# Scales of the last eight quads by way of ScalarE and GpSimd, in a GRU with block attention

## The chip, the cores and the metric

One core of one Trainium2 chip. The metric is the device time of one execution in microseconds; three runs of the kernel before took 367.89, 368.22 and 368.25 us, median 368.22 us.

## The reference, cut to what matters

```
x = x + GRU(initial_state=cond, inputs=x)           # 32 sequences b, 64 steps t, 512 channels
# layer 1, with the blocks of 8 steps summed to 8 keys per sequence:
attn     = softmax(scores of the 8 block sums)      # one weight per block
attended = sum over blocks of attn * block sum      # one vector per b
y        = x + attended @ Wo.T                      # the same vector cp for every t of one b
out      = x + (y - mean(y)) / sqrt(var(y) + 1e-6) * ln_gamma + ln_beta
```

The variance of `y` over the 512 channels of a token is taken from three parts: the sum of squares of the centred `x` (`s2`), twice the product of `x` with the centred `cp`, summed over the channels (the cross sum), and a constant per sequence from `cp` alone (`cp_const`, which holds epsilon too). The scale of a token is that sum to the power -0.5.

## The kernel before, in words

The 64 steps are taken in 16 quads of 4 steps (`Q` = 4, `NQ` = 16); 4 steps by 32 sequences fill the 128 partitions. Up to 336 us the core runs the recurrence, with the input projections of later quads between the steps. Behind the last step comes the tail of some 28 us to which the change belongs: the last block's key and weight, `cp`, and then for each quad one row of output. Every engine has its own program, in order, and the semaphores (`wait_ge`, `then_inc`) tie them together; nothing reorders them.

The quads' scales are computed in three parts (`parts_i`, L114): part 0 holds quads 0 to 3, part 1 quads 4 to 7, part 2 quads 8 to 15. For each part:

- TensorE, `cross_sums` (L771): 16 matmuls per four quads into a bank (`cross_ps[part]`; `keys_ps` for part 2, 128x256).
- VectorE, `cross_own_sums` (L1187): one instruction takes two times the bank by the mask `tok_of_b` (own sequence only), a reduction sums over b. `cross_part` (L1204): that sum by `inv_d` plus `s2` gives `var`.
- ScalarE, `root` (L568): square root with the bias `cp_const`.
- VectorE, `inverse` (L1213) and `spread_rstd` (L213): reciprocal, and the scales spread by the mask into `rstd_of`.
- TensorE, `lay_rstd` (L782): turns the scales into a column per quad (`fourth_ps`), which ScalarE, `keep_rstd` (L576), copies to `rstd_tok`; `add_gcp` (L790) adds the scaled `cp` to the output banks, and needs `rstd_of` too.

For each quad TensorE transposes `x` into an output bank (`lay_x1`, L715; six banks in turn, so quad q waits until VectorE has finished quad q-6), and VectorE's `finish` (L1221) computes the output row in `gcx`, waiting for `u_laid` (the bank is complete) and `rstd_kept`. SyncE stores each row (L324 to L327).

The order of the tail on TensorE is written out in L799 to L839: part 2's cross sums, `lay_s2`, quads 4 and 5, `lay_rstd(1)`, quads 6 and 7, `add_gcp(1)`, quads 8 and 9, `lay_rstd(2)`, quads 10 and 11, `add_gcp(2)`, and so on. That of VectorE stands in L1230 to L1255: `finish(0)` to `finish(3)`, then part 2's scales, `centre_tokens(15)`, then `finish(4)` to `finish(15)`. ScalarE's is in L583 to L593. GpSimd has nothing after its last power, L384.

```
            finish(3)
            cross_own_sums(2)
            cross_part(2)
            inverse(2)
            spread_rstd(dve, 2)
            centre_tokens(NQ - 1)
            for quad in range(Q, NQ):
                finish(quad)
```

Of the kernel before, what the change touches and what calls it, by code (L numbers as in the profile page):

```python
# [8 lines left out]
ALU = mybir.AluOpType  # L9
# [4 lines left out]
P = 128  # L14
# [10 lines left out]
def gru_block_attention(nc, x_tok_d, x_t_d, cond_d, w_ih_d, w_hh_d, bias_d, recs_d, rows_d, wk_t_d,  # L25
# [3 lines left out]
    with ctx:  # L29
# [6 lines left out]
        def sem(name):  # L36
            return ctx.enter_context(nc.semaphore(name))
# [124 lines left out]
            sem("gcp_laid"), sem("gcp_kept"), sem("cross_laid"), sem("cross_step"))  # L162
        var_ready, std_ready, rstd_ready, rstd_spread, rstd_laid, rstd_kept = (
            sem("var_ready"), sem("std_ready"), sem("rstd_ready"), sem("rstd_spread"), sem("rstd_laid"), sem("rstd_kept"))
        u_laid, out_ready, out_stored = sem("u_laid"), sem("out_ready"), sem("out_stored")

        def wait(eng, s, value):
# [45 lines left out]
        def spread_rstd(eng, part):  # L213

            owns = parts_i[part]
            cols, size = slice(owns[0] * Q, (owns[-1] + 1) * Q), len(owns)
            mask = tok_of_b[:].rearrange("p (b t) -> p b t", t=Q)[:, None].broadcast_to([P, size, B, Q])
            scale = rstd[:, cols].rearrange("p (i t) -> p i t", i=size)[:, :, None].broadcast_to([P, size, B, Q])
            eng.tensor_tensor(rstd_of[:, owns[0] * P:(owns[-1] + 1) * P].rearrange("p (i b t) -> p i b t", i=size, t=Q),
                              mask, scale, ALU.mult).then_inc(rstd_spread, 1)  # L220

        block = ctx.enter_context(nc.Block())

# [107 lines left out]
        @block.gpsimd  # L331
        def _(pool):
            pool.memset(bias_rows, 0.0).then_inc(bias_cleared, 1)
            pool.memset(own_rows, 0.0).then_inc(own_made, 1)
            own = own_rows[0:2 * NJ, :].rearrange("p (j b) -> p j b", j=NJ)
            for half_ in range(2):

                pool.wait_ge(own_made, 1 + half_)
                pool.affine_select(out=own, in_=own, compare_op=ALU.not_equal, fill=1.0, base=-NJ * half_,
                                   pattern=[[-1, NJ], [0, B]], channel_multiplier=1).then_inc(own_made, 1)  # L340
            pool.wait_ge(own_made, 3)
            pool.memset(ident[:], 0.0).then_inc(made, 1)
            pool.memset(same_b[:], 0.0).then_inc(made, 1)
            pool.memset(tok_of_b[:], 0.0).then_inc(made, 1)
            pool.memset(own_n[:], 0.0).then_inc(made, 1)
            pool.memset(half[:], -0.5).then_inc(made, 1)
            pool.memset(key_ss[:], 0.0).then_inc(made, 1)
            pool.memset(key_dot[:], 0.0).then_inc(made, 1)
            pool.memset(sums_of, 1.0).then_inc(made, 1)

            pool.wait_ge(made, 8)
            pool.affine_select(out=ident[:], in_=ident[:], compare_op=ALU.not_equal, fill=1.0, base=0,
                               pattern=[[-1, P]], channel_multiplier=1).then_inc(made, 1)
            for g in range(NJ):
                rows = slice(g * B, (g + 1) * B)
                v = same_b[rows, :].rearrange("p (j b) -> p j b", j=NJ)
                w = tok_of_b[rows, :].rearrange("p (b t) -> p b t", t=Q)

                pool.wait_ge(made, 9 + 3 * g)
                pool.affine_select(out=v, in_=v, compare_op=ALU.not_equal, fill=1.0, base=0,  # L360
                                   pattern=[[0, NJ], [-1, B]], channel_multiplier=1).then_inc(made, 1)
                pool.wait_ge(made, 10 + 3 * g)
                pool.affine_select(out=w, in_=w, compare_op=ALU.not_equal, fill=1.0, base=0,
                                   pattern=[[-1, B], [0, Q]], channel_multiplier=1).then_inc(made, 1)
                pool.wait_ge(made, 11 + 3 * g)
                pool.memset(own_n[rows, g:g + 1], 1.0).then_inc(made, 1)

            def save_block(nb):

                wait(pool, br_ready, nb + 1)  # L370
                pool.tensor_copy(br_all[:, bass.ds(nb * P, P)], br_cur[:])
                pool.tensor_copy(br_t[:, :, bass.ds(nb * B, B)],
                                 br_turned[:].rearrange("p (k b) -> p k b", k=NJ)).then_inc(br_saved, 1)

            with pool.Fori(1, NB) as i:
                save_block(i - 1)

            for group in range(2):

                pool.wait_ge(key_var_ready, group + 1)  # L380
                pool.tensor_tensor(key_rms[:, group:group + 1], key_ss[:, group:group + 1], half[:, 0:1], ALU.pow
                                   ).then_inc(key_rms_ready, 1)
            pool.wait_ge(last_var_ready, 1)
            pool.tensor_tensor(last_rms, last_var, half[:, 0:1], ALU.pow).then_inc(last_rms_ready, 1)  # L384
        @block.scalar
        def _(act):
            def split_x(quad):
# [48 lines left out]
            def token_stats(quad, trash=third_ps[:]):  # L436

                wait(act, x1_ready, quad + 1)
                act.activation(trash, gcx_of(quad), ACT.Copy, scale=-1.0 / D, accum_out=column(x_mean, quad)
                               ).then_inc(mean_ready, 1)  # L440
                wait(act, mean_ready, quad + 1)
                act.activation(trash, gcx_of(quad), ACT.Square, bias=column(x_mean, quad),
                               accum_out=column(s2_tok, quad)).then_inc(s2_ready, 1)
# [124 lines left out]
            def root(part):  # L568

                owns = parts_i[part]  # L570
                cols = slice(owns[0] * Q, (owns[-1] + 1) * Q)
                act.wait_ge(cp_const_ready, 1)
                act.wait_ge(var_ready, part + 1)
                act.activation(rstd[:, cols], var[:, cols], ACT.Sqrt, bias=cp_const[:, 0:1]).then_inc(std_ready, 1)
# [11 lines left out]
            keep_rstd(0)  # L586
            root(1)
            token_stats(NQ - 1, stats_trash)
            act.wait_ge(s2_laid, 2)
            move_s2(NQ - Q, Q, fourth_ps, 4 * Q)  # L590
            keep_rstd(1)
            root(2)
            keep_rstd(2)  # L593

        @block.tensor
        def _(pe):
# [184 lines left out]

            def lay_rstd(part):  # L782

                pe.wait_ge(rstd_spread, part + 1)
                for i in parts_i[part]:
                    mm = pe.matmul(fourth_ps[:, P + i * Q:P + (i + 1) * Q], rstd_of[:, i * P:(i + 1) * P],
                                   own_n[:], start=True, stop=True, skip_group_check=True)
                mm.then_inc(rstd_laid, 1)
# [53 lines left out]
        def _(dve):  # L842
# [344 lines left out]
            def cross_own_sums(part):  # L1187

                owns = parts_i[part]
                cols = slice(owns[0] * Q, (owns[-1] + 1) * Q)  # L1190
                size = len(owns)
                own = cross_own[:, 0:size * P]
                dve.wait_ge(cross_laid, part + 1)
                wait(dve, cross_step, 2 * part)
                dve.scalar_tensor_tensor(out=own.rearrange("p (i c) -> p i c", i=size),
                                         in0=cross_ps[part][:, 0:size * P].rearrange("p (i c) -> p i c", i=size),
                                         scalar=2.0, in1=tok_of_b[:, None, :].broadcast_to([P, size, P]),
                                         op0=ALU.mult, op1=ALU.mult).then_inc(cross_step, 1)
                dve.wait_ge(cross_step, 2 * part + 1)
                dve.tensor_reduce(cross[:, cols].rearrange("p (i t) -> p i t", i=size),  # L1200
                                  own.rearrange("p (i b t) -> p i t b", i=size, t=Q), AX.X, ALU.add
                                  ).then_inc(cross_step, 1)

            def cross_part(part):  # L1204

                cols = slice(parts_i[part][0] * Q, (parts_i[part][-1] + 1) * Q)
                dve.wait_ge(cross_step, 2 * part + 2)
                dve.wait_ge(s2_moved, (1, 1, 2)[part])
                dve.wait_ge(denom_step, 3)
                dve.scalar_tensor_tensor(out=var[:, cols], in0=cross[:, cols], scalar=inv_d, in1=s2[:, cols],  # L1210
                                         op0=ALU.mult, op1=ALU.add).then_inc(var_ready, 1)
# [34 lines left out]
            split_s2(NQ - Q, NQ)  # L1246
            finish(2)
            finish(3)
            cross_own_sums(2)
            cross_part(2)  # L1250
            inverse(2)
            spread_rstd(dve, 2)
            centre_tokens(NQ - 1)
            for quad in range(Q, NQ):
                finish(quad)  # L1255
# [46 lines left out]
```

## Time and profile before

| | |
|---|---|
| median of 3 runs | 368.22 us (367.89 to 368.25) |
| the profiled execution, its own time | 368.15 us |
| its span, first to last instruction | 366.3 us |
| granted TensorE clock, mean | 1.0 |
| TensorE busy | 358.6 us, 98% of the span |
| VectorE busy | 263.6 us, 72% |
| ScalarE busy | 166.4 us, 45% |
| GpSimd busy | 11.7 us, 3% |

The profiled execution took 1.85 us more than its span (368.15 against 366.3); this lies around the instructions. Times in the rows are counted from the start of the span. In a row of a timeline stand the start, the time from the first to the last record of the group, the engine, the line of the kernel, the operation, the tensor written and those read, the shape, and the count; in square brackets stands the idle time of the engine before it and what ended it. `gcx` holds the output rows; the tail's small tensors (`cross_own`, `rstd_of`, `var`) lie inside `w_hh`, which the recurrence no longer needs, and `s2` inside `b_in`, so the rows name these.

### The profile page before, as it was taken

What the parts mean: (1) busy time and instruction counts of PE and PEld (TensorE: products, weight loads), DVE (VectorE), ACT (ScalarE), POOL (GpSimd) and SP (SyncE); (2) the same over time, 40 slices, a digit from 0 to 9 for tenths busy, and PEclk for the clock granted to TensorE, in tenths of its full rate; (3) what the DMA queues carried; (4) which work ended last, traced back from release to release, by engine and by line L of the source; (5) the groups of instructions that cost most, each with busy time, mean ns of one, the idle gap of its engine ahead of it and who ended that gap; (6) DMA issues with size and microseconds to landing.
All of it is one profiled execution on the core that took longest, in us unless ns stands there. A gap on an engine that the chain in (4) does not pass through costs nothing.

```text
span 366.3 us, 9562 instructions
## 1 busy us (share of the span) xinstructions
PE 358.6 (98%) x3096; PEld 185.4 (51%) x3096; DVE 263.6 (72%) x1129; ACT 166.4 (45%) x525; POOL 11.7 (3%) x46
## 2 busy tenths in 40 slices
PE   8999999999999999999999999999999999999995
PEld 4545555444555544555544555544555544434772
DVE  3827767677777767776768767776867676888886
ACT  4852236252625343442626262534445255857430
POOL 6000000000000000000000000000000000000000
PEclk9999999999999999999999999999999999999999
DMA  7952625323232322223132323232222312211138
GB/s 309 420 185 73 195 93 166 91 64 88 86 86 86 86 72 72 86 60 112 43 100 57 86 86 86 84 88 64 77 88 57 111 42 69 71 29 30 31 140 320
DMA packets 36275, 38.35 MB, mean 105 GB/s; under 512 B 3992, under 2 KB 27672, under 8 KB 36256
## 3 DMA queue, kind: packets, MB, share of 16 engines
q1 hardware_dynamic: 36240, 38.09, 33.5%
q8 instruction: 11, 0.18, 0.2%
q14 instruction: 8, 0.07, 0.1%
q10 hardware_dynamic: 16, 0.02, 0.0%
HBM read 17.91 MB, written 4.19 MB: 60 GB/s over the span
## 4 chain that ended last, share of the span: by engine, by line
PE 86%; DMA 5%; DVE 3%; issue 3%; SPq 1%; ACT 0%; DVEq 0%; POOLq 0%; POOL 0%; ACTq 0%
PE gates_ps L648 43%; PE gi_ps L616 36%; DMA w_hh<-in_w_hh_dram 2%; DMA gcx<-in_w_ih_dram 2%; PE gi_ps L630 1%; PE fourth_ps L648 1%; PE third_ps L648 1%; PE keys_ps L648 1%; DMA h_tok<-hist 1%; PE gi_ps L729 1%; DVE gcx L1226 0%; PE small_ps L795 0%; SPq L283 0%; DVEq L29 0%; PE small_ps L729 0%
## 5 line engine op out<-in xcount | busy, mean ns | idle before, releaser
L648 PE MATMUL gates_ps<-w_hh,turned 128*32 128x384 f32 x1920 | 167.3, 489 | 0.4 <-DVE turned L875 0.3
L648 PEld LDWEIGHTS gates_ps<-w_hh,turned 128*32 128x32 f32 x1920 | 56.4, 109 | 90.5 <-issue 48.8
L493 ACT ACTIVATE rz<-gates_ps 128x256 f32<-128x256 f32 x59 | 22.7, 384 | 129.1 <-PE gates_ps L648 129.1
L616 PE MATMUL gi_ps<-w_ih_hi,xt_hi 128*128 128x512 f32 x180 | 76.4, 427 | 0.0
L616 PE MATMUL gi_ps<-w_ih_lo,xt_hi 128*128 128x512 f32 x180 | 70.5, 394 | 0.0
L616 PE MATMUL gi_ps<-w_ih_hi,xt_lo 128*128 128x512 f32 x180 | 69.5, 389 | 0.0
L937 DVE TENSOR_TENSOR rz<-gates_ps,rz 128x128 f32<-128x128 f32 x59 | 17.2, 291 | 72.1 <-ACT rz L493 72.0
L616 PEld LDWEIGHTS gi_ps<-w_ih_hi,xt_hi 128*128 128x128 f32 x180 | 33.6, 187 | 42.3 <-issue 36.8
L616 PEld LDWEIGHTS gi_ps<-w_ih_hi,xt_lo 128*128 128x128 f32 x180 | 33.8, 188 | 7.7
L875 DVE STREAM_TRANSPOSE turned<-hist 128x32 f32<-128x32 f32 x189 | 36.1, 216 | 2.1
L616 PEld LDWEIGHTS gi_ps<-w_ih_lo,xt_hi 128*128 128x128 f32 x180 | 33.8, 188 | 5.4 <-issue 0.6
L869 DVE TENSOR_TENSOR hist<-zh,n 128x32 f32<-128x32 f32 x189 | 33.6, 201 | 2.5 <-DVE n L862 0.2
L854 DVE TENSOR_TENSOR gi_tok<-gi_ps,b_in 128x512 f32<-128x512 f32 x45 | 30.7, 683 | 0.0
L862 DVE SCALAR_TENSOR_TENSOR n<-rz,n 128x32 f32<-128x32 f32 x189 | 30.4, 188 | 0.0
L502 ACT ACTIVATE n<-n 128x32 f32<-128x32 f32 x126 | 28.5, 257 | 2.2 <-DVE n L944 1.7
L417 ACT ACTIVATE gates_ps<-bhh_n 128x128 f32<-128x128 f32 x60 | 16.9, 282 | 21.4 <-DVE rz L937 21.4
L426 ACT ACTIVATE gates_ps<-gi 128x256 f32<-128x256 f32 x60 | 22.2, 370 | 0.0
L944 DVE TENSOR_TENSOR n<-rz,gi 128x32 f32<-128x32 f32 x118 | 21.3, 222 | 0.4
L453 ACT ACTIVATE x1t<-x1t,beta_t (+1 forms) x64 | 20.2, 386 | 0.0
L881 DVE TENSOR_TENSOR x1t<-x1t,turned 128x512 f32 (+1 forms) x15 | 16.5, 1103 | 1.9
L945 DVE TENSOR_TENSOR zh<-rz,hist 128x96 f32<-128x96 f32 x63 | 15.8, 251 | 0.0
L391 ACT ACTIVATE xt_hi<-x1t 128x512 fp32r (+1 forms) x15 | 9.4, 629 | 9.0 <-PE gi_ps L616 9.0
(232 smaller groups left out, 295.8 us busy)
## 6 DMA issues: line engine op xcount, KB each, us to landing
gi<-gi_tok SPq DMA_DIRECT2D x60, 128.0 KB, 3.0
x1t<-in_x_t_dram SPq DMA_DIRECT2D x16, 256.0 KB, 2.7
gcx<-in_x_tok_dram SPq DMA_DIRECT2D x16, 256.0 KB, 2.8
h_tok<-hist SPq DMA_DIRECT2D x64, 64.0 KB, 2.1
out_dram<-gcx SPq DMA_DIRECT2D x16, 256.0 KB, 2.1
gi<-gi_tok SPq DMA_DIRECT2D x60, 64.0 KB, 2.2
gcx<-in_w_ih_dram SPq DMA_DIRECT2D x4, 768.0 KB, 6.7
w_hh<-in_w_hh_dram SPq DMA_DIRECT2D x4, 768.0 KB, 9.4
```

The source lines that it names most:

```text
L426: act.activation(gates_ps[:, P:3 * P], gi[:, (s // Q) % 2, first + P:first + G3], ACT.Copy).then_inc(seeded, 1)
L453: ins = act.activation(tile[:, k, :], tile[:, k, :], ACT.Identity, bias=beta_t[:, k * B:k * B + 1])
L493: act.activation(rz[:], gates_bank(t)[:, P:3 * P], ACT.Sigmoid).then_inc(rz_ready, 1)
L502: act.activation(n[:, c], n[:, c], ACT.Tanh).then_inc(n_ready, 1)
L616: mm = pe.matmul(gi_ps[tok][:], a[:, k, :], chunk_cols(w[:, k, :], c), start=(m % 12 == 0), stop=(m % 12 == 11))
L648: mm = pe.matmul(gates_bank(t)[j * B:(j + 1) * B, P:], before[:, k * B:(k + 1) * B], chunk(w_hh, k, j), start=False, stop=(k == NJ - 1), s ...
L854: dve.tensor_tensor(chunk_rows(gi_tok[:, tok, :], c), chunk_rows(gi_ps[tok][:], c), chunk_cols(b_in[:], c), ALU.add).then_inc(gi_tok_ready, 1)
L862: dve.scalar_tensor_tensor(out=n[:, c], in0=z[:, c], scalar=1.0, in1=n[:, c], op0=ALU.subtract, op1=ALU.mult).then_inc(terms_ready, 1)
L869: dve.tensor_tensor(hist[:, s, c], zh[:, c], n[:, c], ALU.subtract).then_inc(h_ready, 1)
L875: dve.transpose(turned[:, s, c], hist[:, s, c]).then_inc(ht_ready, 1)
L937: dve.tensor_tensor(r, bank[:, 3 * P:], r, ALU.mult).then_inc(rh_ready, 1)
L944: dve.tensor_tensor(n[:, c], r[:, c], i_n[:, c], ALU.add).then_inc(n_pre_ready[number], 1)
```

## The change

Parts 0 and 1 stay as they are. For part 2 (quads 8 to 15) the work is laid out anew:

- ScalarE copies the bank of cross sums, by 2, into `cross_own[:, P:3P]` in SBUF (`late_copied`), in its program behind the sums of squares of the last quad and ahead of the move of `s2`.
- GpSimd multiplies it by the mask in place (128x256), adds `cp_const` to `s2` into `var` (128x8), and after VectorE's sums takes the power -0.5 of `cross` into `rstd` (128x8) and spreads it into `rstd_of` (128x256, `late_spread`).
- VectorE keeps the sum over b (`tensor_reduce`, `late_summed` 1) and one instruction, `cross * inv_d + var` (`late_summed` 2). Its product with the mask, its reciprocal and its spread go.
- ScalarE's `root(2)` goes. TensorE's `lay_rstd(2)` waits for `late_spread`.

```diff
@@ gpsimd @@
             pool.tensor_tensor(last_rms, last_var, half[:, 0:1], ALU.pow).then_inc(last_rms_ready, 1)
+
+            late_own, late_cols = cross_own[:, P:3 * P], slice(2 * Q, 4 * Q)
+            pool.wait_ge(late_copied, 1)
+            pool.tensor_tensor(late_own.rearrange("p (i c) -> p i c", i=2), late_own.rearrange("p (i c) -> p i c", i=2),
+                               tok_of_b[:, None, :].broadcast_to([P, 2, P]), ALU.mult).then_inc(late_step, 1)
+            pool.wait_ge(s2_moved, 2)
+            pool.wait_ge(cp_const_ready, 1)
+            pool.tensor_tensor(var[:, late_cols], s2[:, late_cols], cp_const.broadcast_to([P, 2 * Q]), ALU.add
+                               ).then_inc(late_step, 1)
+            pool.wait_ge(late_summed, 2)
+            pool.tensor_tensor(rstd[:, late_cols], cross[:, late_cols], half[:], ALU.pow).then_inc(late_step, 1)
+            pool.wait_ge(late_step, 3)
+            spread_rstd(pool, 2)
@@ scalar @@
             token_stats(NQ - 1, stats_trash)
+            act.wait_ge(cross_laid, 3)
+            act.activation(cross_own[:, P:3 * P], cross_ps[2][:, 0:2 * P], ACT.Copy, scale=2.0).then_inc(late_copied, 1)
             act.wait_ge(s2_laid, 2)
             move_s2(NQ - Q, Q, fourth_ps, 4 * Q)
             keep_rstd(1)
-            root(2)
             keep_rstd(2)
@@ tensor, lay_rstd @@
-                pe.wait_ge(rstd_spread, part + 1)
+                if part == 2:
+                    pe.wait_ge(late_spread, 1)
+                else:
+                    pe.wait_ge(rstd_spread, part + 1)
@@ vector @@
             finish(3)
-            cross_own_sums(2)
-            cross_part(2)
-            inverse(2)
-            spread_rstd(dve, 2)
+            dve.wait_ge(late_step, 1)
+            dve.tensor_reduce(cross[:, 2 * Q:4 * Q].rearrange("p (i t) -> p i t", i=2),
+                              cross_own[:, P:3 * P].rearrange("p (i b t) -> p i t b", i=2, t=Q), AX.X, ALU.add
+                              ).then_inc(late_summed, 1)
+            dve.wait_ge(late_summed, 1)
+            dve.wait_ge(late_step, 2)
+            dve.scalar_tensor_tensor(out=cross[:, 2 * Q:4 * Q], in0=cross[:, 2 * Q:4 * Q], scalar=inv_d,
+                                     in1=var[:, 2 * Q:4 * Q], op0=ALU.mult, op1=ALU.add).then_inc(late_summed, 1)
             centre_tokens(NQ - 1)
```

VectorE's program before, from `finish(3)` to `finish(5)` (L1226 is `finish`, L898 `centre_tokens`):

```order
L1226 SCALAR_TENSOR_TENSOR gcx<-gcx,w_hh,gi_ps 128x512 [waits rstd_kept,u_laid,gcx_ready]
L1195 SCALAR_TENSOR_TENSOR w_hh<-keys_ps,tok_of_b 128x256 [waits cross_step,cross_laid]
L1200 TENSOR_REDUCE w_hh<-w_hh 128x8 [waits cross_step]
L1210 SCALAR_TENSOR_TENSOR w_hh<-w_hh,b_in 128x8 [waits denom_step,s2_moved,cross_step]
L1218 RECIPROCAL w_hh<-w_hh 128x8 [waits std_ready]
L219 TENSOR_TENSOR w_hh<-tok_of_b,w_hh 128x256 [waits rstd_ready]
L898 SCALAR_TENSOR_TENSOR gcx<-gcx,x_mean,tok_consts 128x512 [waits s2_ready]
L1226 SCALAR_TENSOR_TENSOR gcx<-gcx,w_hh,gates_ps 128x512 [waits rstd_kept,u_laid,gcx_ready]
```

and with the change (line numbers of the changed file: L1246 is `finish`, L918 `centre_tokens`):

```order
L1246 SCALAR_TENSOR_TENSOR gcx<-gcx,w_hh,gi_ps 128x512 [waits rstd_kept,u_laid,gcx_ready]
L1270 TENSOR_REDUCE w_hh<-w_hh 128x8 [waits late_step]
L1275 SCALAR_TENSOR_TENSOR w_hh<-w_hh 128x8 [waits late_step,late_summed]
L918 SCALAR_TENSOR_TENSOR gcx<-gcx,x_mean,tok_consts 128x512 [waits s2_ready]
L1246 SCALAR_TENSOR_TENSOR gcx<-gcx,w_hh,gates_ps 128x512 [waits rstd_kept,u_laid,gcx_ready]
```

Five instructions between two outputs' finishes and ahead of `centre_tokens` became two. They wait for GpSimd (`late_step`) in place of TensorE's bank and ScalarE's root.

GpSimd's program from its first power to its end, with the change (before, it ended with the row of L386):

```order
L383 TENSOR_TENSOR b_in<-key_ss,half 128x1 [waits key_var_ready] x2
L386 TENSOR_TENSOR w_hh<-w_hh,half 128x1 [waits last_var_ready]
L390 TENSOR_TENSOR w_hh<-w_hh,tok_of_b 128x256 [waits late_copied]
L394 TENSOR_TENSOR w_hh<-b_in,w_hh 128x8 [waits cp_const_ready,s2_moved]
L397 TENSOR_TENSOR w_hh<-w_hh,half 128x8 [waits late_summed]
L221 TENSOR_TENSOR w_hh<-tok_of_b,w_hh 128x256 [waits late_step]
```

The last four are new; the third of them is a power over eight columns, and the last one is what `lay_rstd(2)` waits for.

## Rows read from the trace of the kernel before

**Rows 1.** The page, part 4: the chain that ended last, shares of the span by engine.

```profile
PE 86%; DMA 5%; DVE 3%; issue 3%; SPq 1%; ACT 0%; DVEq 0%; POOLq 0%; POOL 0%; ACTq 0%
```

**Rows 2.** The chain that ended last, in order of time: start us, us, what.

```profile
355.79 0.66 PE gates_ps L729 x4
...
356.45 0.66 PE gi_ps L729 x4
...
361.63 0.66 DVE gcx L1226
```

**Rows 3.** Timeline of VectorE (DVE): start us, us, engine, line, operation, out<-in, count.

```profile
351.34 0.74 DVE L1226 SCALAR_TENSOR_TENSOR gcx<-gcx,w_hh,gi_ps 128x512 f32<-128x512 f32 x1
351.99 0.42 DVE L1195 SCALAR_TENSOR_TENSOR w_hh<-keys_ps,tok_of_b 128x256 f32<-128x256 f32 x1
352.44 0.61 DVE L1200 TENSOR_REDUCE w_hh<-w_hh 128x8 f32<-128x256 f32 x1
353.09 0.23 DVE L1210 SCALAR_TENSOR_TENSOR w_hh<-w_hh,b_in 128x8 f32<-128x8 f32 x1
353.75 0.20 DVE L1218 RECIPROCAL w_hh<-w_hh 128x8 f32<-128x8 f32 x1 [0.43 <-ACT w_hh L574]
...
354.33 0.75 DVE L898 SCALAR_TENSOR_TENSOR gcx<-gcx,x_mean,tok_consts 128x512 f32<-128x512 f32 x1
354.99 0.74 DVE L1226 SCALAR_TENSOR_TENSOR gcx<-gcx,w_hh,gates_ps 128x512 f32<-128x512 f32 x1
...
363.09 0.74 DVE L1226 SCALAR_TENSOR_TENSOR gcx<-gcx,w_hh,gi_ps 128x512 f32<-128x512 f32 x1
```

**Rows 4.** Timeline of TensorE (PE); a matmul has two passes, each a record.

```profile
348.46 1.96 PE L776 MATMUL keys_ps<-x1t,w_hh 128*32 128x128 f32 x64
...
351.99 0.39 PE L786 MATMUL fourth_ps<-own_n,w_hh 128*128 128x4 f32 x2
...
353.24 0.69 PE L795 MATMUL gates_ps<-w_hh 32*128 32x512 f32 x1
...
353.77 0.59 PE L795 MATMUL gates_ps<-w_hh 32*128 32x512 f32 x1
...
355.24 0.51 PE L786 MATMUL fourth_ps<-own_n,w_hh 128*128 128x4 f32 x4
...
357.03 0.69 PE L795 MATMUL small_ps<-w_hh 32*128 32x512 f32 x1
```

**Rows 5.** Busy time by stretch: engines, granted clock (PEclk), DMA share and GB/s.

```profile
353.80:356.50 2.70, 2.65 (x25) 1.82 (x17) 2.67 (x6) 0.18 (x1) 0.00 (x0) 1.00 0.00 0
359.90:365.40 5.50, 2.43 (x14) 1.16 (x12) 3.79 (x6) 0.00 (x0) 0.00 (x0) 1.00 1.00 376
```

**Rows 6.** The page, part 5: ACT's plain copy of 128x256; busy us, mean ns of one.

```profile
L426 ACT ACTIVATE gates_ps<-gi 128x256 f32<-128x256 f32 x60 | 22.2, 370 | 0.0
```

**Rows 7.** Timeline of ScalarE (ACT), the move of the squares out of fourth_ps.

```profile
351.25 0.69 ACT L479 ACTIVATE b_in<-fourth_ps 32x4 f32<-32x4 f32 x4 [0.96 <-PE fourth_ps L670]
```

**Rows 8.** Timeline of GpSimd (POOL), the whole span: start us, us, then as rows 3.

```profile
3.04 0.09 POOL L349 MEMSET sums_of<- 128x4 f32 x1
...
3.71 0.30 POOL L360 TENSOR_SCALAR_AFFINE_SELECT same_b<-same_b 32x128 f32<-32x128 f32 x1
4.16 0.52 POOL L363 TENSOR_SCALAR_AFFINE_SELECT tok_of_b<-tok_of_b 32x128 f32<-32x128 f32 x1
...
76.72 0.29 POOL L371 COPY br_all<-br_cur 128x128 f32 x1 [68.07 <-DVE br_cur L907]
...
334.44 0.55 POOL L381 TENSOR_TENSOR b_in<-key_ss,half 128x1 f32<-128x1 f32 x1 [9.15 <-DVE key_ss L1023]
341.25 0.71 POOL L384 TENSOR_TENSOR w_hh<-w_hh,half 128x1 f32<-128x1 f32 x1 [6.25 <-DVE w_hh L1150]
```

**Rows 9.** Timeline of VectorE beside the two last GpSimd powers.

```profile
334.29 0.60 DVE L1030 TENSOR_TENSOR b_in<-b_in,turned 128x128 f32<-128x128 f32 x2
...
341.16 0.69 DVE L1154 TENSOR_TENSOR x1t<-x1t,turned 128x128 f32<-128x128 f32 x2
```

More of the change, by code:

```diff
@@ L164, in gru_block_attention @@
             sem("var_ready"), sem("std_ready"), sem("rstd_ready"), sem("rstd_spread"), sem("rstd_laid"), sem("rstd_kept"))
+        late_copied, late_summed, late_step, late_spread = (
+            sem("late_copied"), sem("late_summed"), sem("late_step"), sem("late_spread"))
         u_laid, out_ready, out_stored = sem("u_laid"), sem("out_ready"), sem("out_stored")
@@ L219, in spread_rstd @@
             eng.tensor_tensor(rstd_of[:, owns[0] * P:(owns[-1] + 1) * P].rearrange("p (i b t) -> p i b t", i=size, t=Q),
-                              mask, scale, ALU.mult).then_inc(rstd_spread, 1)
+                              mask, scale, ALU.mult).then_inc(late_spread if part == 2 else rstd_spread, 1)
         block = ctx.enter_context(nc.Block())
```

## The prediction

> **What bounds the kernel now.** I read the chain that ended last first, since the change touches only the tail. Over the whole span 86% of the chain is TensorE and 3% VectorE [rows 1], so VectorE's instructions count only where TensorE waits for them. In order of time the chain of the tail shows two such places: TensorE starts quads 10 and 11's transposes at 355.79 and 356.45, 0.66 us apart, the pace of VectorE's finishes, and at the very end it passes to VectorE at 361.63 [rows 2]. Next the engines' timelines. VectorE ends `finish(3)` and then spends 351.99 to 354.99, 3.00 us, on part 2's scales and on `centre_tokens(15)` before `finish(4)` starts [rows 3]. `finish(4)` ends at 354.99 + 0.74 = 355.73, and TensorE, which needs the bank of quad 4 for quad 10, starts that one 0.06 later, at 355.79 [rows 2, 3]. TensorE had begun `lay_rstd(2)` at 355.24, and reaches `add_gcp(2)` at 357.03 [rows 4]. Call that last time A. Behind A nothing of TensorE waits again: the chain is TensorE's own until 361.63 [rows 2], so the end moves as A does. The output stores are no bound of their own: the DMA engines were idle from 353.8 to 356.5, and from 359.9 to 365.4 they ran at share 1.00 and 376 GB/s [rows 5]. These 5.5 us are the last eight stores, 0.69 each, just above the 0.66 from one finish to the next. If A comes earlier, the stores start earlier and the streak moves with them.
>
> **VectorE's part.** Before, from `finish(3)` to `finish(4)`, from start to start: product 0.45, reduction 0.65, `var` and the wait for ScalarE's root 0.66, reciprocal and spread 0.58, centring 0.66, sum 3.00 [rows 3]. After: the reduction 0.65, one small instruction of 0.23 or 0.25 with its gap, centring 0.66, sum 1.56. So VectorE could start `finish(4)` at 353.55. It can't: quad 4's bank is complete only when the second pass of `add_gcp(1)` ends at 353.77 + 0.59 = 354.36 [rows 4], which the change doesn't touch. With the hand-over of some 0.06 to 0.09, `finish(4)` starts at 354.45, 0.54 earlier than now. Of 1.44 us taken off VectorE 0.90 turn into a wait for TensorE.
>
> **TensorE's part.** With quad 4 finished at 354.45 + 0.74 = 355.19 and quad 5 at 355.85, quads 10 and 11 no longer wait. What is then between `lay_rstd(2)` and A is work alone. The same sequence for part 1 took 353.24 - 351.99 = 1.25 us, with one product fewer in `lay_rstd` (0.39 against 0.51, so 0.12 more) [rows 4]: 1.37 us. If R is the start of `lay_rstd(2)`, A = R + 1.37. TensorE itself gets there at 355.24 as before, so A is at best 356.61, 0.42 us before 357.03. This is the most that the change can bring: 0.11% of the time. A difference below 0.2% (0.74 us) is about what a measurement of this kernel cannot tell from no change.
>
> **ScalarE's part.** Part 2's cross sums end at 348.46 + 1.96 = 350.42 [rows 4]. ScalarE's new copy starts at 350.48 and takes 0.37, by the copy of the same 128x256 [rows 6]: it ends at 350.85, and the move of `s2` queued behind it starts only at 351.25 [rows 7]. It costs nothing; the cover is 0.40 us, and beyond that it would push the move, GpSimd's add and `lay_rstd(1)`, which waits for `s2_moved`. The root that goes ran while ScalarE had nothing else: no gain there beyond VectorE's wait already counted.
>
> **GpSimd's part** decides whether R stays at 355.24. No row shows a 256-column product or a power of more than one column there. For 256 columns the ends are: two copies of 128 (0.29 each, of which 0.09 is what the smallest memset takes), 0.09 + 2 * 0.20 = 0.49; and two selects of L363, whose inner rows are of four elements like those of the spread, 0.09 + 2 * 0.43 = 0.95 [rows 8]. I take 0.75 for the mask and 0.85 for the spread, nearer the select. Mask: 350.91 to 351.66, at worst 351.86; VectorE wants it at 351.99, so it is hidden, with 0.13 to 0.3 us of cover. The add waits for the squares, moved by 351.25 + 0.69 = 351.94 [rows 7], and even at the 0.55 of a one-column power ends by 352.55; VectorE wants it at 352.64. Then the path, all of it exposed towards R: VectorE's small instruction ends at 352.64 + 0.23 = 352.87; GpSimd starts the power at 352.93; the power; 0.15 for its wait on itself (4.16 - 4.01) [rows 8]; the spread 0.85; 0.06 to TensorE. R = 354.0 + the power.
>
> The power over eight columns lies between 0.55 (the shorter one-column power, all of it start-up) and 0.09 + 8 * 0.62 = 5.05 (each column as the longer one, 0.71) [rows 8]. The row it is nearest to is the one-column power, and the copy shows an engine whose cost sits mostly at the start (128 columns for 0.20). I choose 0.71 + 7 * 0.07 = 1.2 us. R would be 355.19, just in time: A = 356.61, gain 0.42. The profiled execution's 368.15 becomes 367.73; it stood 0.07 under the median of 368.22, so the median becomes **367.8**. The slack is only 0.05 us: any later R comes off the gain one for one until it is zero at R = 355.66 (a power of 1.67 us), and a loss beyond. With the low ends (0.55 and 0.49) nothing more is won, since TensorE is not ready earlier.
>
> For the 256-column product there is also a page. The Trainium skill, "GPSIMD Engine Reference", section 3.1 on elementwise work, gives some 2.6 cycles an element at 1.2 GHz for two inputs; an estimate from it is 0.56 us plus dispatch, and by it R would be some 0.2 us earlier and the sum the same. No run here shows it yet.
>
> **The rivals.**
>
> - *The power is paid by the column* (slower). Place: `lay_rstd(2)` waits for `late_spread`, and behind it stand quads 10 to 15. At 0.31 a column (half of the first one's 0.62) it takes 2.57, R = 356.56, A = 357.93, +0.90: 369.1. At the full 0.62 a column, 5.05, R = 359.05, A = 360.42, +3.4: 371.6. It decides from 1.67 us (0.20 a column) on, and gives more than 0.74 us of loss from 2.41 us (0.29 a column). For it: one column costs six times a memset [rows 8]. Against: nothing but the copy's small cost by the column. Chance 0.32, of it 0.28 beyond 0.74 us.
> - *The power is held up by VectorE's centring.* `centre_tokens(15)` starts at 352.89 with two inputs from SBUF, 0.75 us long [rows 3], and the power starts 0.04 behind it. The trace shows a power beside two-input VectorE work twice: once 0.71, once 0.55 [rows 8, 9], so a hold of 0.16 or none. If the power were held until the centring ends at 353.64, it would be 0.71 later in place of the 0.16 counted: R = 355.74, A = 357.11, +0.08: 368.3. Chance 0.11. The Trainium skill, "SBUF — State Buffer", section "Who interferes with whom", says that a VectorE instruction with two SBUF inputs contends with a GpSimd one that reads SBUF, and that who comes second waits for the whole of the first. By that rule the time is this rival's; the 0.55 us power at 334.44, started 0.15 us into such work, speaks against a full hold, and the 0.71 us one for a partial one.
> - *The gain is larger than 0.74 us.* It would take TensorE at `lay_rstd(2)` earlier than 355.24, and no instruction of it before that waits for anything the change moves. Chance 0.04, for what the rows don't show.
> - *Nothing moves*, since GpSimd's other pieces eat the 0.42 (the 0.95 ends, a hand-over of 0.2 more): within 0.1 of 368.2. Chance 0.03.
>
> **How the numbers follow.** The forecast, a gain of 0.1 to 0.45, has the remaining 0.50. Faster by over 0.2%: 0.04. Slower: 0.28 from the first rival and 0.01 from the second, 0.29. Within 0.2%: 0.67. The forecast's own range is 367.7 to 368.1, with 0.1 either way for the measurement. The range for 8 in 10 starts at 367.5 and must reach into the first rival: up to 370.3, a power of 3.7 us (0.45 a column), beyond which I leave some 0.13.
>
> **What would show it.** In the changed profile: VectorE's two instructions from 351.99 to 352.9, `centre_tokens` to 353.6, then an idle stretch of 0.9 us until `finish(4)` at 354.45; ScalarE's copy at 350.5; GpSimd's four instructions, the third of 1.2 us and the last ending by 355.2; `lay_rstd(2)` at 355.24, quads 10 and 11 no longer on a pace of 0.66, `add_gcp(2)` at 356.6; a span of 365.9. I am wrong if the power is over 1.7 us (then TensorE sits idle ahead of `lay_rstd(2)` and a wait for GpSimd enters the chain), or if the mask ends after 352 and VectorE waits behind `finish(3)`. No idle stretch on VectorE ahead of `finish(4)` would refute my reading of what binds it.

## The result, and the profile after

The changed kernel took 368.78 us (median of 22 runs, 368.35 to 371.22); the kernel before, in the same sessions, 368.30 us (22 runs, 367.81 to 370.69). The ratio of after to before is 1.0021, with a 95% interval of 1.0012 to 1.0030: slower by 0.1 to 0.3%, 0.4 to 1.1 us. The forecast was 367.8 us, a gain of 0.1%. The time lies in the range of 367.5 to 370.3 that was given, but on the other side of no change.

The profiled execution of the changed kernel took 370.27 us with a span of 368.1 us. It is one of the slower ones of the 22: its input loads came late, the first recurrent step starts 1.99 us later than before, and the tail stands 1.47 us later. So I count the tail from one instruction that the change doesn't touch, the start of `lay_s2` on TensorE: 350.82 before, 352.29 after.

The chain's shares by engine, from the page (before: [rows 1]):

```profile
PE 90%; DVE 4%; DMA 2%; POOL 1%; issue 1%; ACT 1%; DVEq 0%; POOLq 0%; SPq 0%; ACTq 0%
```

GpSimd (POOL) is in it now. The same chain in order of time, its part in the tail (start us, us, what):

```profile
353.55 0.54 DVE w_hh L1270
...
354.11 0.24 DVE w_hh L1275
...
354.41 2.09 POOL w_hh L397
...
356.55 0.66 POOLq L29
...
357.34 0.58 PE fourth_ps L806 x4
357.92 0.49 PE gates_ps L746 x4
358.42 0.44 PE gi_ps L746 x4
```

The chain of before had TensorE here without a break, with two transposes on VectorE's pace [rows 2]. Now it runs from VectorE's reduction over the power on GpSimd (L397) and the spread to `lay_rstd(2)` (L806), and the two transposes behind it are 0.49 and 0.44 us, TensorE's own.

GpSimd's timeline in the changed kernel:

```profile
352.40 0.73 POOL L390 TENSOR_TENSOR w_hh<-w_hh,tok_of_b 128x256 f32<-128x256 f32 x1 [8.98 <-ACT w_hh L606]
353.49 0.20 POOL L394 TENSOR_TENSOR w_hh<-b_in,w_hh 128x8 f32<-128x8 f32 x1 [0.35 <-ACT b_in L495]
354.41 2.09 POOL L397 TENSOR_TENSOR w_hh<-w_hh,half 128x8 f32<-128x8 f32 x1 [0.73 <-DVE w_hh L1275]
356.58 0.62 POOL L221 TENSOR_TENSOR w_hh<-tok_of_b,w_hh 128x256 f32<-128x256 f32 x1
```

Mask and spread take 0.73 and 0.62 us, the add 0.20, and the power over eight columns 2.09, where I had put 1.2.

VectorE, ScalarE and TensorE around it:

```profile
353.46 0.61 DVE L1270 TENSOR_REDUCE w_hh<-w_hh 128x8 f32<-128x256 f32 x1
354.11 0.23 DVE L1275 SCALAR_TENSOR_TENSOR w_hh<-w_hh 128x8 f32<-128x8 f32 x1
354.25 0.74 DVE L918 SCALAR_TENSOR_TENSOR gcx<-gcx,x_mean,tok_consts 128x512 f32<-128x512 f32 x1
355.92 0.75 DVE L1246 SCALAR_TENSOR_TENSOR gcx<-gcx,w_hh,gates_ps 128x512 f32<-128x512 f32 x1 [0.93 <-DVE gcx L918]
...
360.00 0.75 DVE L1246 SCALAR_TENSOR_TENSOR gcx<-gcx,w_hh,small_ps 128x512 f32<-128x512 f32 x1 [1.35 <-PE gi_ps L815]
```

```profile
351.94 0.38 ACT L606 ACTIVATE w_hh<-keys_ps 128x256 f32<-128x256 f32 x1 [0.19 <-PE keys_ps L793]
352.72 0.69 ACT L495 ACTIVATE b_in<-fourth_ps 32x4 f32<-32x4 f32 x4 [0.39 <-PE fourth_ps L687]
```

```profile
352.29 0.40 PE L687 MATMUL fourth_ps<-b_in 128*128 128x16 f32 x2 [0.41 <-DVE b_in L1102]
...
357.34 0.58 PE L806 MATMUL fourth_ps<-own_n,w_hh 128*128 128x4 f32 x4 [0.47 <-POOL w_hh L221]
...
358.78 0.69 PE L815 MATMUL small_ps<-w_hh 32*128 32x512 f32 x1
```

VectorE's part came as forecast: no wait behind `finish(3)`, the centring at once, then 0.93 us idle ahead of `finish(4)`, which starts 3.63 us behind `lay_s2` in place of 4.17 [rows 3], the 0.54 of the prediction. ScalarE's copy of 0.38 us is over 0.40 us before its next work. But TensorE starts `lay_rstd(2)` 5.05 us behind `lay_s2` instead of 4.42, with a wait for GpSimd ahead of it, and `add_gcp(2)` at 6.49 instead of 6.21. From there all goes on as before: the last finish comes at +12.55 (before +12.27), and the span ends at +15.81 (before +15.52). The tail lost 0.28 us.

This is under half of 0.77 us, the 0.21%. The other part is not in the span. In the 22 runs of the changed kernel the time less the span is 2.16 us in the median (2.09 to 2.22). In the profiled execution of before it was 1.81 (1.85 if the span is taken as 366.3), and in the 35 runs of before that stand beside the first experiments 1.81 too (1.77 to 1.87), so that no run of the one kernel comes near one of the other. The edit adds some 0.33 us outside the span, which the prediction had taken as fixed. Both parts together are 0.6 us, within the interval of 0.4 to 1.1.

### The profile page after: what moved, and what is told of

It is laid out like the page before. It is cut to its first block, busy times and chain, and to the rows that moved or that the text cites. A ratio compares the mean times of both kernels' runs of the same rounds, so it can differ in the third digit from the quotient of the medians.

```text
span 368.1 us, 9562 instructions
## 1 busy us (share of the span) xinstructions
PE 359.7 (98%) x3096; PEld 185.4 (50%) x3096; DVE 262.4 (71%) x1126; ACT 166.4 (45%) x525; POOL 15.6 (4%) x50
## 4 chain that ended last, share of the span: by engine, by line
PE 90%; DVE 4%; DMA 2%; POOL 1%; issue 1%; ACT 1%; DVEq 0%; POOLq 0%; SPq 0%; ACTq 0%
PE gates_ps L665 44%; PE gi_ps L633 37%; DMA gcx<-in_bias_dram 1%; PE gi_ps L647 1%; PE first_ps L716 1%; DVE gcx L1246 1%; PE fourth_ps L665 1%; PE third_ps L665 1%; PE keys_ps L665 1%; PE first_ps L665 1%; PE fourth_ps L716 1%; PE third_ps L716 1%; PE keys_ps L716 1%; DMA h_tok<-hist 1%; POOL w_hh L397 1%
## 5 line engine op out<-in xcount | busy, mean ns | idle before, releaser
L965 DVE TENSOR_TENSOR zh<-rz,hist 128x96 f32<-128x96 f32 x63 | 15.8, 250 | 0.0
L373 POOL COPY br_all<-br_cur 128x128 f32 x7 | 2.0, 293 | 305.2 <-DVE br_cur L927 305.2
```

## The experiments

Two questions: what holds `lay_rstd(2)`, and where the 0.33 us outside the span come from. In the table, "out" is the time less the span; it and the span are medians of the kernel's runs; the last three columns are from the one profiled execution of each kernel, counted from the start of `lay_s2`.

| kernel | GpSimd instructions | runs | span | out | `lay_rstd(2)` | `add_gcp(2)` | end of span |
|---|---|---|---|---|---|---|---|
| before (profiled; runs beside the first four) | 46 | 35 | 366.4 | 1.81 | +4.42 | +6.21 | +15.5 |
| changed | 50 | 22 | 366.65 | 2.16 | +5.05 | +6.49 | +15.8 |
| e1_sem4 | 46 | 12 | 366.5 | 1.83 | +4.42 | +6.23 | +15.5 |
| e2_reuse | 50 | 11 | 366.7 | 2.14 | +5.05 | +6.49 | +15.8 |
| e3_mult | 50 | 11 | 366.0 | 2.15 | +4.42 | +5.79 | +15.1 |
| e4_order | 46 | 11 | 365.9 | 1.81 | +4.42 | +5.79 | +15.1 |
| f1_early4 | 50 | 11 | 366.3 | 2.04 | +4.42 | +6.23 | +15.6 |
| f2_late1 | 47 | 11 | 366.5 | 1.95 | +4.42 | +6.23 | +15.5 |
| f4_late_mult | 47 | 11 | 366.4 | 1.98 | +4.43 | +6.23 | +15.5 |
| f3_widths | 54 | 10 | 366.4 | 1.81 | +5.05 | +6.49 | +15.8 |
| g1_pad | 54 | 11 | 366.8 | 1.80 | +5.06 | +6.50 | +15.8 |
| g2_centre | 50 | 11 | 366.2 | 2.19 | +4.62 | +6.06 | +15.4 |
| g3_centre_pad | 54 | 11 | 366.4 | 1.79 | +4.62 | +6.06 | +15.4 |
| g4_early8 | 54 | 11 | 366.8 | 1.81 | +4.42 | +6.22 | +15.5 |

Each ratio below compares a kernel with runs of before from its own session. Beside the f kernels before had 368.29 us, a span of 366.5 and 1.82 outside; beside the g kernels 368.00, 366.2 and 1.83.

The tail and the time outside repeat to some hundredths. What is left of the span, from its start to `lay_s2`, does not (350.6 to 351.3 in these profiles, 352.3 in that of the changed kernel): it is where a median of eleven runs gets its scatter of 0.2 to 0.4 us.

### Spare semaphores (e1_sem4)

```diff
+        spare = [sem(f"spare{k}") for k in range(4)]
```

> The kernel before with four more semaphores that nothing uses; no instruction differs. The tail of the changed kernel ends only 0.28 us later than before (counted from the same instruction), while the 22 runs each say 0.21% (0.77 us). Theory A: the rest lies outside the span and belongs to the four new semaphores; this kernel is then slower than before by 0.2 to 0.4 us, its span unchanged, its time outside the span 2.15 in place of 1.85 us. Rival B: the rest is chance in the loads at the start; this kernel is then within 0.1 us of before in both.

Measured: 368.34 us, ratio 1.0009 (0.9995 to 1.0023), time outside the span 1.83. The rival's number: semaphores are not the cause, my first theory fell. But chance in the loads, which the rival named, isn't the cause of the 0.33 us either: the loads lie in the span, and the 0.33 us outside it.

### The change without new semaphores (e2_reuse)

```diff
-            pool.wait_ge(late_copied, 1)
+            pool.wait_ge(warmed, 3)
...
-            pool.wait_ge(late_summed, 2)
+            pool.wait_ge(cross_step, 6)
...
-                    pe.wait_ge(late_spread, 1)
+                pe.wait_ge(rstd_spread, part + 1)
```

GpSimd's steps are counted on `made`, VectorE's sums on `cross_step` in the same way.

> The changed kernel with its four new semaphores replaced by counts on existing ones, the instructions and their order the same. Theory A: the time outside the span falls back to 1.85 us and the kernel is 0.28 us (0.08%) slower than before, that is 0.3 us faster than the changed kernel. Rival B: it is as slow as the changed kernel.

Measured: 368.82 us, ratio 1.0011 (1.0002 to 1.0020), outside 2.14: as the changed kernel, tail and all. What costs the 0.33 us is in the instructions.

### A product in place of the power (e3_mult)

```diff
-            pool.tensor_tensor(rstd[:, late_cols], cross[:, late_cols], half[:], ALU.pow).then_inc(late_step, 1)
+            pool.tensor_tensor(rstd[:, late_cols], cross[:, late_cols], half[:], ALU.mult).then_inc(late_step, 1)
```

> The changed kernel with the power over eight columns replaced by a product over the same operands, so the scales of the last eight quads are not the reference's. Theory 'the power is the late link' expects GpSimd's third instruction to take 0.2 us as its add does in place of 2.09, lay_rstd(2) to start 1.56 us behind the start of quad 8's... more exactly at TensorE's own pace with no wait for GpSimd, and add_gcp(2) 0.63 us earlier than in the changed kernel, so 0.6 us less in the span and 0.35 us less than before in the tail. Rival: if the spread or the hand-overs of GpSimd were the late link, a wait for GpSimd stays ahead of lay_rstd(2).

This kernel leaves the power out, so its output is not the reference's; it is there for its times. Measured: 368.18 us, ratio 0.9998 (0.9990 to 1.0007), with the 2.15 us outside. GpSimd's timeline:

```profile
352.18 0.20 POOL L394 TENSOR_TENSOR w_hh<-b_in,w_hh 128x8 f32<-128x8 f32 x1 [0.35 <-ACT b_in L495]
353.10 0.64 POOL L397 TENSOR_TENSOR w_hh<-w_hh,half 128x8 f32<-128x8 f32 x1 [0.73 <-DVE w_hh L1275]
353.82 0.62 POOL L221 TENSOR_TENSOR w_hh<-tok_of_b,w_hh 128x256 f32<-128x256 f32 x1
```

`lay_rstd(2)` is back at +4.42 and `add_gcp(2)` at +5.79, 0.70 us before the changed kernel's and 0.42 before that of before: all that the prediction said the change could bring. So the spread and the hand-overs are not the late link; the third instruction is. And it shows a second thing: the product over eight columns takes 0.64 us here, while the add over as many columns, with as many inputs, takes 0.20. Beside the product VectorE runs `centre_tokens(15)`, which reads two operands from SBUF; beside the add it doesn't. A product of the same shape stands at the end of GpSimd's program in f4_late_mult below, where VectorE only finishes outputs, with one operand from SBUF and one from PSUM:

```profile
355.89 0.20 POOL L386 TENSOR_TENSOR w_hh<-w_hh,half 128x8 f32<-128x8 f32 x1 [13.88 <-PE fourth_ps L788]
```

So it isn't the product: the 0.44 us are a hold, a time in which GpSimd's instruction is under way but waits for VectorE's. My forecast of 0.2 us for this kernel's third instruction missed it.

### The order on VectorE alone, in the kernel before (e4_order)

```diff
             cross_part(2)
+            centre_tokens(NQ - 1)
             inverse(2)
             spread_rstd(dve, 2)
-            centre_tokens(NQ - 1)
```

> The kernel before with one line moved: centre_tokens(15) ahead of inverse(2) on VectorE, in the time in which it waits for ScalarE's root. My account of what binds TensorE expects the wait of 0.43 us ahead of the reciprocal gone, finish(4) at some 354.5 counted as before, quads 10 and 11 without a wait, and add_gcp(2) 0.35 to 0.42 us earlier: 0.1% faster than before, as much as the change could have brought at best. If TensorE is held by something else there, no gain.

Measured: 367.71 us (367.30 to 368.21) beside 368.26 for before, ratio 0.9988 (0.9979 to 0.9997). VectorE's timeline:

```profile
353.00 0.23 DVE L1210 SCALAR_TENSOR_TENSOR w_hh<-w_hh,b_in 128x8 f32<-128x8 f32 x1
353.15 0.75 DVE L898 SCALAR_TENSOR_TENSOR gcx<-gcx,x_mean,tok_consts 128x512 f32<-128x512 f32 x1
353.81 0.20 DVE L1218 RECIPROCAL w_hh<-w_hh 128x8 f32<-128x8 f32 x1
354.04 0.42 DVE L219 TENSOR_TENSOR w_hh<-tok_of_b,w_hh 128x256 f32<-128x256 f32 x1
354.38 0.74 DVE L1226 SCALAR_TENSOR_TENSOR gcx<-gcx,w_hh,gates_ps 128x512 f32<-128x512 f32 x1
```

The 0.43 us of waiting for ScalarE's root [rows 3] are filled with the centring, `finish(4)` starts when its bank is complete, and `add_gcp(2)` stands at +5.79. One moved line, with nothing given to ScalarE or GpSimd, has the whole gain. It is the fastest kernel of this study, and the only one whose interval lies wholly on the side of a gain.

### More instructions on GpSimd, early or late (f1_early4, f2_late1, f4_late_mult)

f1: `memset(key_ss)` in two pieces, `memset(sums_of)` in four, at the start of GpSimd's program. f2 and f4, behind its last power:

```diff
+            pool.wait_ge(rstd_laid, 3)
+            pool.memset(stats_trash[:, 0:1], 0.0)
```

with this as the last line in f4:

```diff
+            pool.tensor_tensor(stats_trash[:, 0:2 * Q], var[:, 2 * Q:4 * Q], half[:], ALU.mult)
```

> The kernel before with two of GpSimd's memsets at the start split into six, so that its program has four instructions more, as in the changed kernel, but none late. In the changed kernel and both of its variants the time outside the span was 2.14 to 2.16 us, against 1.81 in before, in the one with spare semaphores and in the reordered one. Theory 'count': it is the length of GpSimd's program; here the time outside the span is then 2.1 us or more. Theory 'late': it is that GpSimd still works in the tail; here it stays 1.8 us.

> The kernel before with one memset of one column on GpSimd that waits for the last scales to be laid (rstd_laid 3), into memory that nobody reads. Theory 'late': the time outside the span goes to 2.1 us. Theory 'count' (four instructions): it stays near 1.8. The span stays 366.4.

> As the one before, with a product of 128x8 with two inputs in place of the memset. A third theory, 'kind': only an instruction like the new ones (two inputs, read from SBUF) late in the tail costs the 0.33 us outside the span. It is then at 2.1 us here and at 1.8 with the memset.

Measured outside the span: 2.04 with four more early, 1.95 with one memset late, 1.98 with one product late; ratios 0.9996 (0.9983 to 1.0009), 1.0003 (0.9994 to 1.0013) and 1.0008 (0.9995 to 1.0021). Early instructions cost outside the span too, so "late" falls, and memset and product are alike, so "kind" falls. What is left is that it has to do with how long GpSimd's program is, but not in proportion.

The records of instruction transfers in the traces tell more. Instructions reach the core in blocks; those of the queue q14 have 8 KB. The last ones of each trace, in us from the start of the span (for f3 and the g kernels see the next two sections):

```
kernel          GpSimd instr.  span     last 8 KB transfers of q14 (start)    out
before               46        366.34   315.6, 343.5                          1.81
e1_sem4              46        366.52   315.7, 343.7                          1.83
e4_order             46        365.81   315.5, 343.4                          1.81
f2_late1             47        366.56   316.1, 343.7                          1.95
f4_late_mult         47        366.43   316.0, 343.6                          1.98
changed              50        368.09   317.0, 345.0,          369.6          2.16
e2_reuse             50        366.86   315.8, 343.7,          368.3          2.14
e3_mult              50        366.07   316.1, 343.7,          367.6          2.15
f1_early4            50        366.34   315.5, 343.5,          368.2          2.04
g2_centre            50        366.00   315.4, 343.3,          367.5          2.19
f3_widths            54        366.91   316.2, 343.8, 353.0                   1.81
g1_pad               54        366.67   315.9, 343.6, 352.5                   1.80
g3_centre_pad        54        366.38   315.8, 343.7, 353.0                   1.79
g4_early8            54        366.79   316.0, 343.5, 344.0                   1.81
```

With four instructions more on GpSimd, one more block is fetched, 1.5 to 1.9 us behind the end of the span, whatever they are and wherever they stand. In the changed kernel it is the only transfer of any queue from 369 to 371 us (the DMA view of that window):

```profile
DMA packets 1, 0.01 MB, mean 4 GB/s; under 512 B 0, under 2 KB 0, under 8 KB 0
q14 instruction: 1, 0.01, 1.8%
```

With eight more the block is already fetched within the span. The kernels with the late block are those with 2.04 to 2.19 us outside. The expectation of g1_pad below puts the late block 12.7 and 13.1 us behind the span. Those times were counted from the start of the recording, 11.2 us ahead of the span; counted like everything else they are 1.5 and 1.9 us. This matters for the reading: some 12 us behind the span the fetch would lie far behind the end of the measured time, which is only 2.2 us longer than the span; 1.5 us behind it, the fetch, 0.31 to 0.57 us long, can lie within.

### The price of a power by its width (f3_widths)

```diff
             spread_rstd(pool, 2)
+            for width in (1, 2, 4, 8):
+                pool.tensor_tensor(stats_trash[:, width - 1:2 * width - 1], var[:, 2 * Q:2 * Q + width], half[:, 0:width], ALU.pow)
```

> The changed kernel with four more powers on GpSimd behind its spread, of 1, 2, 4 and 8 columns of the same input, into memory that nobody reads, while VectorE only finishes outputs (one input from SBUF, one from PSUM). Theory 'by the column': the start and a price a column, 0.55, 0.77, 1.2 and 2.09 us, 0.22 a column, and the power beside the centring was not held up. Rival 'held': the eight columns take 1.4 to 1.7 us here, and the rest of the 2.09 was the wait for the shared interface. Rival 'steps': 8 columns cost hardly more than 4. The time outside the span: 2.14 us by 'late' and 'kind', 2.3 us or more by 'count'.

The groups by line and shape (busy us, mean ns of one); L397 is the change's power, L401 the added ones, beside which VectorE only finishes outputs:

```profile
L397 POOL TENSOR_TENSOR w_hh<-w_hh,half 128x8 f32<-128x8 f32 x1 | 2.1, 2088 | 0.7 <-DVE w_hh L1277 0.7
L401 POOL TENSOR_TENSOR w_hh<-w_hh,half 128x8 f32<-128x8 f32 x1 | 1.6, 1636 | 0.0
...
L401 POOL TENSOR_TENSOR w_hh<-w_hh,half 128x4 f32<-128x4 f32 x1 | 1.0, 1012 | 0.0
...
L401 POOL TENSOR_TENSOR w_hh<-w_hh,half 128x2 f32<-128x2 f32 x1 | 0.7, 702 | 0.0
...
L401 POOL TENSOR_TENSOR w_hh<-w_hh,half 128x1 f32<-128x1 f32 x1 | 0.5, 544 | 0.0
```

544, 702, 1012, 1636 ns: a straight line, 0.39 us and 0.156 us a column. Both of the prediction's slow mechanisms hold at once: the power is paid by the column (1.64 us for eight), and beside the centring it is held for another 0.45 us. The time of the kernel was 368.21 us, ratio 1.0002 (0.9993 to 1.0011), with 1.81 us outside: the changed kernel with four more powers, 3.8 us of GpSimd work, came out nearer to before than the changed kernel did (ratio 1.0021). Both of my forecasts for the time outside, 2.14 and 2.3 us, missed.

### Padding and the centring's place (g1_pad, g2_centre, g3_centre_pad, g4_early8)

g1 is the changed kernel with the split memsets of f1; g4 is before with four memsets split into twelve; g2:

```diff
-            centre_tokens(NQ - 1)
             for quad in range(Q, NQ):
+                if quad == 2 * Q:
+                    centre_tokens(NQ - 1)
                 finish(quad)
```

g3 is g1 and g2 together.

> The changed kernel with two of GpSimd's memsets at the start split into six: eight instructions on GpSimd more than before in place of four. Theory 'instruction block': with four more, the end of GpSimd's program crosses into an 8 KB block of instructions that is fetched only behind the span (in the trace of the changed kernel 12.7 us behind it, in the one with four early memsets 13.1), and with eight more it is fetched within the span, as with the four extra powers. So the time outside the span falls from 2.15 to 1.8 us, and the kernel is 0.3 us faster than the changed one, 368.5, though it does more. Rival 'each instruction costs': the time outside stays at 2.15 us or grows.

> The changed kernel with centre_tokens(15) moved on VectorE from ahead of finish(4) to behind finish(7), so that it no longer runs beside GpSimd's power. Theory 'held': the power over eight columns falls from 2.09 to 1.64 us, lay_rstd(2) starts 0.45 us earlier, and the span is 0.45 us shorter than the changed kernel's, 0.2 us less than before. Rival 'by the column alone': the power stays 2.09 us and the span at 366.7.

> Both edits together. If both theories hold: power 1.64 us, span 366.2, outside it 1.8 us, 368.0 us in all, 0.2 to 0.3 us faster than before. By the rivals it stays at 368.8.

> The kernel before with eight more memsets' instructions on GpSimd at the start (four memsets split into twelve), nothing else. Theory 'instruction block': the time outside the span is 1.8 us as in before, less than the 2.04 with four more. Rival 'each instruction costs': 2.2 us or more.

GpSimd in g2_centre:

```profile
352.75 1.65 POOL L397 TENSOR_TENSOR w_hh<-w_hh,half 128x8 f32<-128x8 f32 x1 [0.73 <-DVE w_hh L1275]
354.47 0.61 POOL L221 TENSOR_TENSOR w_hh<-tok_of_b,w_hh 128x256 f32<-128x256 f32 x1
```

With the centring away, the power takes 1.65 us, `lay_rstd(2)` starts at +4.62 and `add_gcp(2)` at +6.06, 0.43 us before the changed kernel's and 0.15 before that of before. The hold is shown from both sides. In runs g2 has 368.36 us beside 368.00, ratio 1.0013 (1.0004 to 1.0022): the 2.19 us outside cost more than the tail gives. The span's median is 366.2, as before's; the tail's 0.15 us don't show in it.

With padding the time outside is 1.79 to 1.81 in all three kernels, as expected, and the block is fetched in the span (the page counts 9 or 10 blocks of q14 in it, 8 before). Yet none of the padded kernels is faster than before, as g3 was to be: g1 368.61 (1.0011, 0.9995 to 1.0027), g3 368.17 (1.0005, 0.9992 to 1.0018), and g4 is slower than before, 368.61 (1.0010, 1.0001 to 1.0019), with a span of 366.8 beside 366.2 and an unchanged tail. What eight more pieces at the start of GpSimd's program cost ahead of `lay_s2` wasn't found out. In g4's one profile the 0.43 us by which `lay_s2` is late are there before the recurrence is far on (0.45 us at GpSimd's first copy, 77.17 against 76.72), and the chain has the load of `w_hh` end at 21.75 us instead of 21.30; whether the padding does that is not shown. Of my forecasts for these four the tails and the times outside held, and the 368.5 us of g1 came out near; the span of g2, 0.2 us less than before's, and the total of g3, 0.2 to 0.3 us less, did not.

## Why the prediction was wrong

- **What binds the tail: right.** TensorE waited for VectorE's finishes only at quads 10 and 11; `finish(4)` could start 0.54 us earlier and no more; with R the start of `lay_rstd(2)` and A that of `add_gcp(2)`, A = R + 1.37 us; the most to be had is 0.42 us. e3_mult and e4_order show exactly these numbers (+4.42, +5.79 against +6.21). In the changed kernel, where TensorE has to wait ahead of R, R to A took 1.44, with 0.58 for `lay_rstd(2)` in place of 0.51.
- **ScalarE's copy and the mask: right.** 0.38 us for 0.37, hidden with 0.40 us to spare; the mask 0.73 for 0.75, ended at 353.13, and VectorE, ready at 353.46, did not wait.
- **The spread: 0.62 for 0.85**, too dear by 0.23; its inner rows of four elements didn't make it dearer than the mask. The Trainium skill's figure in "GPSIMD Engine Reference", section 3.1, some 2.6 cycles an element, an estimated 0.56 us plus dispatch, was the better guide for it: here the trace agrees for both products of 256 columns, 0.62 and 0.73 us, with 0.06 and 0.17 us left for the dispatch.
- **The power: the step that failed.** The sum had "0.71 + 7 * 0.07 = 1.2 us"; it is 2.09. Alone it is 1.64: a further column costs 0.156, not 0.07. I had let the copy, a nearer shape but not a nearer operation, speak for the price by the column. The point at which the gain turns into a loss had been put at 1.67 us, so by this alone the tail would have come out even; g2_centre, with the power at 1.65 and the spread 0.23 cheaper than in the sum, shows a gain of 0.15.
- **The hold: the rival I gave 0.11 was the mechanism, beside the first.** "A hold of 0.16 or none" was taken from two powers; it is 0.45. The power starts 0.16 us behind the start of the centring (354.41 against 354.25), whose record runs for another 0.58 us. The Trainium skill, "SBUF — State Buffer", section "Who interferes with whom", has it that the second to come waits for the whole of the first. Here the trace agrees in the main: 0.44 us for a product and 0.45 for a power, of those 0.58. It doesn't agree for the first power of [rows 8]: that one started with 0.12 us of a two-input instruction's record to go and took 0.55 us, as did the one at 324.74 beside a reduction, which has one input, so it was not held at all. In [rows 9] the instructions beside were short, so that little was left to wait for; they bound nothing for one of 0.75 us, and I used them as if they did.
- **What lies around the span: a term that the sum did not have.** I moved 368.15 by the change of the span alone. 0.33 us were added outside.

The two rivals were priced as alternatives. Had they been added, 1.64 + 0.45 = 2.09 against the turning point of 1.67, the sum would have given a loss of 0.42 us in the tail. Less the 0.23 by which the spread was cheaper that is 0.19; the rest of the 0.28 measured is mostly the 0.07 us that R to A took longer.

**What stays open.** Whether the block of instructions fetched late is what lengthens the time outside the span is not shown, only that the two go together: five kernels with the late block have 2.04 to 2.19 us outside, seven without it and with 46 or 54 instructions have 1.79 to 1.83. Against a simple wait for it speak that one more instruction (f2, f4) gave 0.13 to 0.16 us without a recorded late block, and that f1's block ends 2.17 us behind the span while its profiled execution has 2.04 outside. Open too is why the span of the kernels with padding at the start is longer.

## What to carry to other kernels

An engine's waiting time is first a place for other work of that same engine: look for an independent instruction in its own queue (here one line) before a chain is laid over other engines. When work goes to GpSimd, price it by the operation and the columns, and look at what VectorE runs beside it: here an instruction with two SBUF inputs held it for 0.45 of the 0.58 us that its record still ran. And at differences of 0.1%, compare the time less the span as well: here the length of one engine's program went with a change of 0.33 us in it, as much as the edit moved the span.

## What was not expected of the hardware

- A power on GpSimd costs 0.39 us and 0.156 us for each column of 128 partitions; a product of 256 columns costs only 0.62 to 0.73.
- A GpSimd instruction of 128x8 that starts 0.16 us behind a VectorE one with two SBUF inputs takes 0.44 to 0.45 us longer than alone: 0.64 for 0.20 us (product), 2.09 for 1.64 (power). The hold stands in its record.
- The time outside the span is 1.8 us with 46 or 54 GpSimd instructions, 1.95 to 1.98 with 47, and 2.04 to 2.19 with 50, there along with an 8 KB block of instructions fetched 1.5 to 1.9 us behind the end of the span.
